# Two batches on the two halves of the partitions in a routed block, started behind the second group of expert tiles

## What is computed

```python
# mixture of experts (all four batches, T = 2048 tokens, 8 experts, two of them per token)
scores = softmax((x @ wt.T + g @ wg.T) / 2);  topk_w, topk_idx = top_k(scores, 2)
gp = leaky(einsum('th,ehm->etm', x, w_gate)); up = einsum('th,ehm->etm', x, w_up)
y_all = einsum('etm,emh->eth', gp * up, w_down)
y = weighted sum of the two chosen experts + leaky(x @ sw_gate) * (x @ sw_up) @ sw_down   # shared experts

# routed block, per batch b of 512 tokens, 16 heads of 16
weights = y @ router_w + router_b
topv, topi = top_k(weights, 64); thr = topv[:, -1]; sel_mask = weights > thr
sel_idx = sort(topi[:, :63])                      # 63 tokens of each batch
x_sel, pos_sel, w_sel = rows, positions and weights of those tokens
m_sel = attention_mask[b, sel_idx][:, sel_idx]
hn = rmsnorm(x_sel, ln1)
q, k = rope(hn @ wq), rope(hn @ wk);  v = hn @ wv
a = softmax(q k^T / 4 + m_sel);  x1 = x_sel + (a v) @ wo
x2 = x1 + gelu(rmsnorm(x1, ln2) @ w1) @ w2        # 256 -> 1024 -> 256
out[sel_idx] = x2 * w_sel;  out = out + y * (1 - sel_mask)
result = x + out
```

## Time and profile before

| | us |
|---|---|
| median of 3 runs | 2619.83 |
| lowest and highest | 2619.05, 2630.92 |
| profiled execution, its own time | 2618.87 |
| its span, first to last instruction | 2617.0 |
| TensorE busy | 2419.8 (92%) |
| VectorE, ScalarE, POOL busy | 1378.5, 1104.8, 1075.6 |
| mean granted clock of TensorE | 0.958 |

### The profile page before, as it was taken

The page is one execution under the profiler, slowest core; times in us unless marked ns, Lnnn a source line. Parts: engine busy times, 40 slices in busy tenths (PEclk is TensorE's granted clock), DMA queues, the critical chain, the costliest instruction groups (busy, mean ns, idle before and its releaser), DMA issues. The chain is left out here.

```text
span 2617.0 us, 38670 instructions
## 1 busy us (share of the span) xinstructions
PE 2419.8 (92%) x13380; PEld 1574.2 (60%) x13380; DVE 1378.5 (53%) x3259; ACT 1104.8 (42%) x2708; POOL 1075.6 (41%) x1119
## 2 busy tenths in 40 slices
PE   7999999899999889799999999999999899878867
PEld 4565655533443357686878778556656567665545
DVE  7466575467777343433324243565655577543563
ACT  4767586344544324211111111464666355333322
POOL 3655465168778333541212121765655200044200
PEclk9999999989999999999999999999999999989776
DMA  4000000000000044410000100442333000533200
GB/s 162 1 1 1 1 1 21 9 13 13 13 11 12 10 146 138 164 41 1 1 1 1 43 1 1 149 122 79 107 101 108 9 1 1 165 99 93 63 19 19
DMA packets 101712, 126.94 MB, mean 49 GB/s; under 512 B 17986, under 2 KB 80203, under 8 KB 101140
## 3 DMA queue, kind: packets, MB, share of 16 engines
q1 hardware_dynamic: 94052, 104.42, 12.7%
q0 software_dynamic: 7472, 20.06, 2.8%
HBM read 102.76 MB, written 17.47 MB: 46 GB/s over the span
## 5 line engine op out<-in xcount | busy, mean ns | idle before, releaser
L1005 POOL TENSOR_TENSOR cb_sc<-cb_toep,cb_mk 128x128 f32<-128x128 f32 (+3 forms) x256 | 215.7, 872 | 187.0 <-ACT cb_pr L1043 177.0
L1005 POOL TENSOR_TENSOR cb_bias<-cb_bias,cb_mk 128x128 f32<-128x128 f32 (+3 forms) x256 | 214.6, 868 | 147.7 <-DMA cb_bias<-in_fside_16xSxS 147.4
L1639 DVE TENSOR_REDUCE gb_bmax<-PS 128x8 f32<-128x512 f32 x256 | 164.6, 684 | 85.9 <-PE PS L1417 85.3
L389 PE MATMUL PS<-ident,cb_pr 128*128 128x128 f32 x1280 | 198.8, 285 | 4.0 <-ACT cb_pr L1043 2.3
L690 DVE CUSTOM_DVE_ANT_0 cb_sc<-PS,cb_sc,cb_sneg 128x128 f32<-128x128 f32 (+3 forms) x256 | 129.9, 547 | 121.9 <-PE PS L379 118.4
L389 PEld LDWEIGHTS PS<-ident,cb_pr 128*128 128x128 f32 x1280 | 135.3, 141 | 96.9 <-issue 82.5
L1798 ACT ACTIVATE gb_pt<-PS 128x512 f32<-128x512 f32 x256 | 139.6, 596 | 110.9 <-PE PS L1424 105.8
L1049 ACT ACTIVATE cb_pt<-PS 128x128 f32<-128x128 f32 (+3 forms) x448 | 163.5, 414 | 38.9 <-PE PS L389 38.3
L1417 PE MATMUL PS<-gb_ks,gb_qs 32*128 32x512 f32 x512 | 170.6, 666 | 8.2 <-DVE gb_bmax L1639 6.7
L690 DVE CUSTOM_DVE_ANT_0 cb_bias<-PS,cb_bias,cb_sneg 128x128 f32<-128x128 f32 (+3 forms) x256 | 129.4, 547 | 91.3 <-PE PS L379 90.3
L2321 PE MATMUL PS<-eb_g,ff_h 128*128 128x256 f32 x768 | 173.6, 379 | 0.0
(11 more groups left out here) (713 smaller groups left out, 5126.8 us busy)
## 6 DMA issues: line engine op xcount, KB each, us to landing
cb_bias<-in_fside_16xSxS SPq DMA_DIRECT2D x64, 256.0 KB, 2.9
cb_bias<-in_fside_16xSxS SPq DMA_DIRECT2D x64, 192.0 KB, 2.5
ff_h<-in_L_ffn_h_w SPq DMA_DIRECT2D x2, 4096.0 KB, 15.9
cb_bias<-in_fside_16xSxS SPq DMA_DIRECT2D x64, 128.0 KB, 2.3
y_group<-eb_ys SPq DMA_DIRECT2D x22, 256.0 KB
y_rows<-eb_g SPq DMA_DIRECT2D x19, 256.0 KB
cb_toep<-rel_table SPq DMA_DIRECT2D x8, 512.0 KB, 6.5
x_rows<-X SPq DMA_DIRECT2D x2, 2048.0 KB, 8.8
```

The costliest lines, as they stand in the source:

```text
L389: ins = pe.transpose(PS[:, bank, j * P:j * P + P], pr[:, v % 2, e, j * P:j * P + P], ident)
L1005: ins = pool.tensor_tensor(biases(v, e), turned(h, n) if L0 else biases(v, e), mk[:, b % 2, packed(t):packed(t) + n], ALU.add)
L1639: dve.tensor_reduce(bmax[:, n % 2, t, g + e, 0:NB], PS[:, bank + e, :].rearrange("p (n k) -> p n k", k=64), AX.X, ALU.max)\
```

## The change

Two parts. First the routed block runs on a pair q of batches: batch 2q in partitions 0 to 63, batch 2q+1 in 64 to 127. `xs`, the norms, the rotation, the scores' softmax, `hidden` and `processed` are done once for a pair. Products that must stay apart by batch (`chosen_rows`, `chosen_mask`, `token_scores`, `mix_values`, `back_to_rows`) are issued for each half h, with `tile_position` in columns or rows 64h. `turn_queries`, `hidden` and `turn_probabilities` fill 2, 2 and 4 banks for a pair, where they filled 1, 1 and 2 for a batch. Second the order: nothing of the block but batch 0's weights, counts and choice is done inside the tiles of group 1; `into(3, *)` and `down(3)` move behind them; POOL's returns are cut up between the gathers of group 1, and the gather of the mask's rows for the first pair stands between the returns of batch 2 and 3. Several tensors now lie in rooms that are free by then.

```diff
-        hots, A = sb("hot", [P, 2, NT, KSEL]), sb("A", [P, NT, R])
+        hots, A = sb("hots", [P, GB, NT, P]), sb("A", [P, NT, P])
...
+        part = lambda h: slice(KSEL * h, KSEL * h + KSEL)
...
+                def chosen_rows(ring, q):
+                    bank = ring.put(pe, ("xs", q))
+                    pe.wait_ge(sm["rc_S"], GB * q + GB)
...
                     for t in range(NT):
-                        ins = pe.matmul(PS[0:KSEL, bank, 0:YW], hot_of(b)[:, t, :], Y[:, b * NT + t, :], start=(t == 0),
-                                        stop=(t == NT - 1))
+                        for h in range(GB):
+                            ins = pe.matmul(PS[part(h), bank, 0:YW], hots[:, q, t, part(h)], Y[:, (GB * q + h) * NT + t, :],
+                                            start=(t == 0), stop=(t == NT - 1), tile_position=(0, KSEL * h))
...
-                        ins = pe.matmul(PS[0:R, bank, h * AV:h * AV + AV], pT[:, i, :], V[:, h, :], start=True, stop=True)
+                        n = HC * (i % HC) + i // HC
+                        for h in range(GB):
+                            ins = pe.matmul(PS[part(h), bank, n * AV:n * AV + AV], pT[:, i, part(h)], V[:, h, n, :], start=True,
+                                            stop=True, tile_position=(0, KSEL * h))
...
+                    for k in range(2):
+                        bank = ring.put(pe, ("h1", q, k))
...
+                        for i in range(KH):
+                            m = KH * k + i
+                            for c in range(DC):
+                                ins = pe.matmul(PS[:, bank, i * P:i * P + P], wr["w1"][:, c, m * P:m * P + P], hnT[:, 1, c, :],
+                                                start=(c == 0), stop=(c == DC - 1))
...
                 into(2, 1)
-                into(3, 0)
-                down(2)
-                into(3, 1)
                 expert_of(1, 0)
                 turn_rows(1, 0)
-                down(3)
+                down(2)
                 for i in range(GP + 1):
                     tiles(1, i)
-                    if i == 2:
+                    if i == 5:
                         turn_y(mixed, 0)
-                    elif i == 3:
+                    elif i == 6:
                         token_weights(mixed, 0)
-                    elif i == 7:
-                        chosen_rows(mixed, 0)
-                        turn_choice(mixed, 0)
...
+                into(3, 0)
                 pair_out(1, GP - 1)
+                into(3, 1)
+                turn_y(late, 1)
+                token_weights(late, 1)
+                down(3)
+                chosen_rows(late, 0)
+                turn_choice(late, 0)
+                turn_normed(late, 0, 0)
+                queries_keys(late, 0)
+                token_values(late, 0)
+                turn_queries(late, 0)
...
+                hidden(late, 0)
+                turn_y(late, 3)
+                token_weights(late, 3)
+                processed(late, 0)
+                back_to_rows(late, 0)
+                back_to_rows(late, 1)
                 chosen_rows(late, 1)
...
```

VectorE's new order behind the tiles, and POOL's:

```diff
+                choice(1)
+                chosen_rows(0)
+                rms(0, 0)
+                normed(0, 0)
+                turn_normed(0, 0)
+                rope(0)
+                combine(2, range(NT))
+                token_scores(0)
+                token_weights(2)
+                own_weights()
+                count(0)
+                count(1)
+                mix_values(0)
...
+                combine(3, range(NT))
+                processed(0)
+                token_weights(3)
+                own_weights()
                 for t in range(NT):
-                    count(1, t)
-                choice(1)
-                mix_values(0)
+                    count(t)
+                choice(3)
                 chosen_rows(1)
                 rms(1, 0)
                 normed(1, 0)
...
+                kept_rows(0)
                 turn_normed(1, 0)
...
+                back_to_rows(0)
                 rope(1)
...
+                kept_rows(1)
+                back_to_rows(1)
                 token_scores(1)
...
-                return_rows(0)
-                gather(1, range(XG, 2 * XG))
-                return_rows(1)
-                gather(1, range(2 * XG, GT))
+                return_rows(0, range(0, 4))
+                gather(1, range(XG, 10))
+                return_rows(0, range(4, 8))
+                gather(1, range(10, 14))
+                return_rows(1, range(0, 2))
+                gather(1, range(14, 18))
+                return_rows(1, range(2, 4))
+                gather(1, range(18, GT))
+                return_rows(1, range(4, 8))
+                stored(1)
+                return_rows(2, range(8))
                 rows_of_mask(0)
-                stored(1)
-                return_rows(2)
-                return_rows(3)
+                return_rows(3, range(8))
                 rows_of_mask(1)
-                rows_of_mask(2)
-                rows_of_mask(3)
```

More of the change, by code:

```diff
@@ L3336, in turn_normed @@
                         at(("xs", q)).wait_emptied(pe, ("xs", q))
-                        ins = pe.matmul(PS[:, bank, DC * R:DC * R + 1], wr["last"][:, :], xs[:, q, D:D + 1], start=True, stop=True)
+                        for h in range(GB):
+                            ins = pe.matmul(PS[:, bank, D + h:D + h + 1], wr["last"][:, h, :], xs[:, q, D:D + 1], start=True,
+                                            stop=True)
                     ins.then_inc(ring.filled(("T", q, k)), 1)
@@ L3428, in processed, with back_to_rows @@
+                        ins = pe.matmul(PS[:, bank, 0:D], g[:, m, :], wr["w2"][:, m, :], start=(m == 0), stop=(m == FC - 1))
                     ins.then_inc(ring.filled(("h2", q)), 1)
-                def back_to_rows(ring, q):
+                def back_to_rows(ring, b):
+                    q, h = b // GB, b % GB
+                    rows = slice(KSEL * h, KSEL * h + R)
                     for half in range(2):
-                        bank = ring.put(pe, ("sc", q, half))
+                        bank = ring.put(pe, ("sc", b, half))
@@ L3508, in tensor_program @@
                 token_values(late, 1)
-                turn_normed(late, 0, 1)
-                hidden(late, 0)
                 turn_queries(late, 1)
                 mask_columns(late, 1)
-                processed(late, 0)
                 chosen_mask(late, 1)
@@ L3516, in tensor_program @@
                 token_scores(late, 1, 1)
-                turn_y(late, 2)
-                back_to_rows(late, 0)
-                token_weights(late, 2)
                 turn_probabilities(late, 1)
-                turn_y(late, 3)
                 mix_values(late, 1)
@@ L3954, in vector_program @@
+                count(1)
+                mix_values(0)
+                count(2)
+                token_out(0)
+                rms(0, 1)
+                normed(0, 1)
+                turn_normed(0, 1)
+                count(3)
+                choice(2)
+                combine(3, range(NT))
+                processed(0)
+                token_weights(3)
+                own_weights()
                 for t in range(NT):
-                    count(1, t)
-                choice(1)
-                mix_values(0)
+                    count(t)
@@ L3960, in vector_program @@
                 normed(1, 0)
-                token_out(0)
-                rms(0, 1)
+                kept_rows(0)
                 turn_normed(1, 0)
-                normed(0, 1)
-                combine(2, range(NT))
-                turn_normed(0, 1)
+                back_to_rows(0)
                 rope(1)
-                processed(0)
+                kept_rows(1)
+                back_to_rows(1)
                 token_scores(1)
-                kept_rows(0)
-                back_to_rows(0)
-                token_weights(2)
-                own_weights()
-                combine(3, range(NT))
                 mix_values(1)
-                for t in range(NT):
-                    count(2, t)
-                choice(2)
                 token_out(1)
```

498 lines of the change are left out of this document (203 added, 295 removed).

## The result

| us | before | changed |
|---|---|---|
| median | 2620.95 (4 runs) | 2579.60 (4 runs) |
| lowest, highest | 2619.05, 2630.92 | 2574.37, 2582.12 |
| profiled execution, its own time | 2618.87 | 2579.63 |
| its span | 2617.0 | 2577.7 |
| TensorE busy | 2419.8 | 2377.6 |

The ratio of changed to before is 0.9832 (95% interval 0.9803 to 0.9861): 41 us less. The forecast was 2573, in a range of 2550 to 2600. Behind line 3080 the two kernels number their lines differently (`mix_values` is line 3395 before and 3413 after, POOL's gather 4253 and 4198), so steps are best found by their names.

The account below looks back on a forecast made before the run. The last stage was taken as a relay between engines, none full, so fewer steps would help. Gains of 24 us ahead and 21 in the relay put the last addition at 2567, span 2571.5, time 2573.4; range 2550 to 2600.

Parts of the forecast that it names:

- parts 1: Ahead of group 1's tiles: `into(3,*)` and `down(3)` move behind the tiles, gaining 10.7 us.
- part 3: From the tiles' end to pair 0's first hot matrix: 20.4 us, with `down(3)` hidden under VectorE's weights, counts and choice.
- Part 5: Up to pair 1's hot matrix: VectorE does `processed(0)`, then batch 3's weights, counts and choice, nearly alone, 9.5 us.
- Part 2: Tiles of group 1: 40 us of work, 9 of stall kept, 3 at the ends, 52 instead of 65.2.
- Part 6: Pair 1, hot matrix to last addition: the same chain with nothing to fill it, 66 us.
- Rival (b): No stall in group 1's tiles: 9 us off, time 2564; chance 15%.
- Part 4: Pair 0's chain from hot matrix to `processed`, each step priced by its row: 50.3 us.
- loads do not overlap: Weight loads in column halves run serially, so `mix_values` saves nothing: 3.9 us warm, 7.0 cold.
- Mostly at 1.2 GHz: Pair 1's chain has nothing to fill it, so TensorE runs mostly at the low clock; warm would take off some 10 us.
- Rival (a): The relay gains nothing, as two pairs do not overlap as four batches did: time 2595; chance 15%.
- Rival (d): Column halves serialize everywhere and the clock stays low in pair 0 too: time 2587; chance 15%.
- Rival (c): Slower: POOL and ScalarE starve each other in the tiles, 3.2 us a copy, loop 154 us: time 2675; chance 3%.

Follow-up runs that it names:

- e1: Changed kernel with only batch 3's shared experts (`into(3, *)`, `down(3)`) put back ahead of group 1's tiles; 2545.6 us, ratio to before 0.9814.
- e3: Changed kernel with steps of batches 2 and 3, `chosen_rows(1)` and batch 3's returns moved earlier; 2526.2 us, ratio to before 0.9744.
- c1: The changed kernel unaltered, run again on a chip where the kernel before took 2601.0 us; 2537.1 us, ratio to before 0.9772.
- c2: The kernel before, unaltered, traced again beside c1; the kernel before had a median of 2601.0 us there.
- e6: e3 with batch 3's weights on TensorE moved behind `token_out`; 2525.8 us, ratio to before 0.9727.
- e2: Changed kernel with all products of one column half issued before the other's, in `chosen_rows`, `chosen_mask` and `mix_values`; one time, 2557.9 us.
- e5: Changed kernel with identity transposes, results overwritten, filling TensorE's waits in pair 1; one time, 2523.6 us.
- e8: Changed kernel with group 1's gathers first, returns behind them, combines, weights and counts of batches 0 and 1 behind the tiles; 2588.1 us once, before at 2624.6.
- e7: e6 with identity transposes filling TensorE's waits in both pairs and batch 2's counts and choice earlier on VectorE; 2552.4 us, ratio to before 0.9729.
- e10: e7 unaltered, run again beside e9 on the same chip; 2558.4 us, ratio to before 0.9733.
- e9: e7 with the mask's gather between the returns of batches 2 and 3 on POOL; 2560.3 us, ratio to before 0.9744.

## Why the prediction was right

The profiled execution against the prediction's own parts:

| part | predicted | measured |
|---|---|---|
| 1, ahead of the tiles | 10.7 less | 10.7 less |
| 2, tiles | 52 | 58.0 |
| 3, to the hot matrix of pair 0 | 20.4 | 19.8 |
| 4, pair 0 | 50.3 | 53.0 |
| 5, VectorE alone | 9.5 | 9.5 |
| 6, pair 1 | 66 | 53.9 |
| behind | 4.4 | 4.8 |
| `into(2, 0)`, moved by unchanged code | 0 | 9.5 later |

The time lies in the range, and the way the gain comes about was forecast: a shorter stretch ahead of the tiles, shorter tiles, and a relay of two chains in place of four. Its sizes were right in parts 1, 3 and 5 and wrong in parts 2 and 6. Of the signs that it named, `hidden` at no more than 7.1 us, VectorE's 9 us ahead of the second `chosen_rows` and some 4.4 us behind the last addition came. Counted from `into(2, 0)`, the first `pair_into` came 10.7 us earlier as named, the last tile 17.9 and not 20 to 25, and `mix_values` at 4 to 7 us failed.

**Parts 1, 3 and 5** held, each to 0.6 us or better, and e1 shows that the order of the shared experts alone is worth 4.4 us: the 10.7 gained ahead are partly paid back in part 3, as the sum had it. Part 5's price is the clearest number of the case: e3 takes it away, for 9 us, together with the wait that it causes. It is a fault of the changed kernel's order, not of the pairs.

**Part 2.** 40 of work and 3 at the ends were right: c1 takes 44.2 with no stall. The stall was taken at 9 and is 13.8. The argument for keeping it (POOL issues without a pause) came true here, but by luck: c1, c2 and e1 to e6 have bursts as long or longer, up to 31 transfers in c1, and no stall. Rival (b), no stall, is what c1 shows: it took 9 off where 13.8 go.

**Part 4** was 2.7 over its 50.3, and 3.8 over its own terms, which add up to 49.2. Weights of batch 2 ran at the low clock ahead of the probabilities (3.75); c1, the same code, has 1.96 there and takes 59.3 for what takes 62.6 here (parts 4 and 5). `mix_values` was 2.04, not 3.9, and the scores 1.09, not 2.6, so the other steps went over by more than that: the probabilities waited 1.3 us behind those weights, the normalization 1.2 behind counts of batch 2 on VectorE, and `hidden` took 6.21, not 5.5.

**Part 6 is the step that failed in size**, by 12.1 us, and two terms of it, worth 6.1 us, share one mistake. `mix_values` was priced at 6.1 from the statement that "loads do not overlap"; it took 2.04 here and 3.60 where the clock was low (e3). The 2.04 lies outside the bounds of 3.9 to 7.0 that the range was built on. The scores stood at 3.1 and took 1.09.

The statement came from the earlier trace rows, 0.034 us for quarters of 32 columns, read as load plus a quarter of the stream; e2 shows what the case was: 0.032 us a product in turns of the halves, 0.062 to 0.068 one half after the other, so the load overlaps as well. Of the 6.1 us some 3.3 are this overlap and the rest the clock (an estimate: 3.9 at the full clock became 2.04, and the 3.1 of the scores, a price at the low clock, took 1.67 in c1 at 0.50). The Trainium skill (TensorE: Matmul & The Clock Gate, Part 3) ties the overlap of a load to another row group, which the two column halves do not have; its rule would have made e2 equal to the changed kernel, and the 2.04 against 4.34 decides against it.

The rest was mostly the clock. "Mostly at 1.2 GHz" was right up to the values (0.50 from 2519 to 2533) and for the probabilities (0.56), and wrong for the scores and the mixing (1.00) and behind them: `hidden` had 0.67 on average, 5.46 us against 7.06, and `processed` ran at 1.00, 3.62 against 6.62. e5 prices what was left of it at 9.2 us. That doubling the stream of `hidden` is free did come out: 32 instructions with 128 columns streamed took 3.84 us at 1.00 (e5), those with 63 took 7.06 at 0.50. The 0.44 us that the prediction quotes for four transposes is the distance between two starts; the row has 0.60.

So the sum, 2573.4, came out 6 us under the 2579.6 by luck, through errors that cancel: 12 too much in pair 1, against 6 too little in the tiles, 2.7 in pair 0 and 9.5 by which this execution reached the stage later. The stage by itself was forecast 45.6 us shorter and became 49.2 shorter. The relay did gain more than the prediction gave it: 167.5 us from the tiles' end became 136.2, 31 us and not 21. Rival (a) falls with that. Rival (d) falls on both counts, halves and clock. Rival (c) did not come true, yet its mechanism exists: with the stall ScalarE stands still for 8 to 11 us in one piece or, before, five copies took 16.6 us; a pace of 3.2 us a copy did not last.

**What stays open.** What ScalarE, VectorE and POOL wait for while POOL's transfers follow one another, and why it happens in all six traces taken beside a kernel before of over 2615 us and in none of the eight beside one of 2601 or less. The rows name no releaser that can be true, and the stall does not always last until the transfers run dry: in e8 they ran on to 2413. No kernel with forced pauses inside the tiles was run. The groups with the stall and those without it ran on different chips, but each chip at one moment only, so whether it belongs to the chip or to the moment is not shown. One rival can be looked at in the trace: an engine that waits for its next instructions to be loaded. The DMA section has two queues of instruction loads; between 2366 and 2399 us of the changed kernel, over the whole stall, neither carried a packet, and the first one behind it landed when ScalarE had already gone on (2395.96). So no recorded load ends the stall; whether the loads of every engine are recorded is not shown.

The change is no part of the cause: the kernel before has the same stall in a stretch that the change leaves alone. ScalarE's timeline in the tiles of group 0, where POOL had issued fourteen gathers in a row in both kernels, first before, then changed:

```profile
2314.93 0.38 ACT L4063 ACTIVATE eb_gs<-PS 128x256 f32<-128x256 f32 x1 [6.98 <-DMA ff_w<-in_L_ffn_w_w]
```
```profile
2326.25 0.39 ACT L4026 ACTIVATE eb_gs<-PS 128x256 f32<-128x256 f32 x1 [7.85 <-DMA ff_w<-in_L_ffn_w_w]
```

The products that the two copies wait for had ended 7 and 8 us before. c2 and c1 have no such wait there, with POOL issuing 23 and 22 transfers in a row.

The best versions are e6, 0.9727 without the stall, where the changed kernel has 0.9772 with an interval that overlaps, and e7, 0.9729 with it, where the changed kernel has 0.9832, clear of it.

## What to carry to other kernels

Two batches on the two halves of the partitions pay in the number of handings-on: products for the pair cost what those for one did (`processed` 3.62 us against 3.67 at the full clock), and those that must stay apart by batch cost half each, if they alternate between the column halves. Where a chain of small steps leaves an engine idle, look at what stands first on VectorE ahead of the next chain (9 us here) and at the granted clock (9 us here) before counting instructions. And look at a stage in traces of more than one chip before believing a stall in one trace: 14 us of the changed kernel's tiles came and went with no edit.

## What the runs showed of the hardware

- 64 products with 63 rows and 64 columns loaded and 17 columns streamed take 2.04 us at 2.4 GHz, alternating between column halves, and 3.60 at the low clock; one half after the other they took 4.34 and 3.95 at a granted clock of 0.82 and 0.91 (e2).
- Transposes of 128 by 128 whose result nobody reads hold the granted clock at 1.00 in a chain whose own work left it at 0.72 (e5 and c1).
- `hidden` in pair 0 and 1 took 3.81 to 6.68 us in the changed kernel and the experiments for the same 32 instructions, by the clock it met; `processed` behind it always 3.62.
- Beside a kernel before of over 2615 us, each burst of 14 to 19 indirect transfers in the tiles of either group went with ScalarE, VectorE or POOL standing still for 3 to 11 us with their input there; behind the tiles bursts of 17 (e7, e10) and 9 (e9) did, one of 17 in the kernel before and one of 9 in the changed kernel did not. Beside a kernel before of 2601 or less bursts of up to 31 did nothing.
